# Distance attention: VectorE's clip as a maximum with a bank of PSUM, and GpSimd's second product without its wait for that clip

## What is computed

```python
scores = einsum('bhid,bhjd->bhij', qh, kh) / sqrt(DH)
p = softmax(where(maskb, scores, -1e32)) * maskb
cum, tot = cumsum(p, -1), sum(p, -1, keepdims=True)
pos = abs(idx[None, :] - idx[:, None])
dist_scores = sqrt(clip((tot - cum) * pos, 0.0, None))
gamma, diff = -softplus(gammas), exp(sigmoid(pdiff))
total_effect = clip(exp(dist_scores * gamma * diff), 1e-05, 100000.0)
scores = where(maskb, scores * total_effect, -1e32)
out = einsum('bhij,bhjd->bhid', softmax(scores), vh)
```

## Time and profile before

| what | us |
|---|---|
| median of 3 runs | 3223.43 |
| lowest, highest | 3220.07, 3230.75 |
| the profiled execution | 3222.4 |
| its span in the profile | 3220.3 |

### The profile page before, as it was taken

The page is one execution under the profiler, slowest core; times in us unless marked ns, Lnnn a source line. Parts: engine busy times, 40 slices in busy tenths (PEclk is TensorE's granted clock), DMA queues, the critical chain, the costliest instruction groups (busy, mean ns, idle before and its releaser), DMA issues. The chain is left out here.

```text
span 3220.3 us, 46152 instructions
## 1 busy us (share of the span) xinstructions
PE 2755.0 (86%) x14900; PEld 1548.8 (48%) x14900; DVE 1879.3 (58%) x4757; ACT 1721.1 (53%) x2884; POOL 852.0 (26%) x957
## 2 busy tenths in 40 slices
PE   7899869959999999556699988999867888888887
PEld 4233349824444454322322257999533444444453
DVE  6677551165555655303688640111569999999963
ACT  3565421146555555101277632333159999999963
POOL 4100020020000000001300021000447888888840
PEclk8899989979999999788899999999987999999989
DMA  5111156510000000694312145999250010000011
GB/s 172 47 51 50 48 180 218 195 58 1 1 1 1 1 1 1 264 423 191 96 49 64 45 157 222 341 348 343 86 174 11 21 27 17 22 21 20 18 30 49
DMA packets 161813, 327.00 MB, mean 102 GB/s; under 512 B 29408, under 2 KB 128480, under 8 KB 138208
## 3 DMA queue, kind: packets, MB, share of 16 engines
q1 hardware_dynamic: 152128, 304.78, 27.0%
q0 software_dynamic: 4608, 12.59, 1.2%
q10 hardware_dynamic: 4896, 7.35, 0.7%
HBM read 275.22 MB, written 49.28 MB: 101 GB/s over the span
## 5 line engine op out<-in xcount | busy, mean ns | idle before, releaser
L2987 DVE TENSOR_TENSOR_SCAN L3x_behind<-L3x_first_exp,L3x_beside_scan 128x513 f32<-128x513 f32 x256 | 309.7, 1210 | 0.0
L2867 POOL TENSOR_TENSOR L3x_fade<-L3x_behind,L3x_apart 128x1024 f32<-128x1024 f32 x128 | 280.8, 2194 | 68.6 <-DVE L3x_behind L2987 45.0
L1320 ACT ACTIVATE L1x_probs<-L1x_scores,L1x_neg_max 128x512 f32<-128x512 f32 x256 | 173.5, 683 | 218.7 <-DVE L1x_neg_max L1372 218.7
L1372 DVE TENSOR_REDUCE L1x_neg_max<-L1x_scores 128x2 f32<-128x1024 f32 x128 | 156.6, 1224 | 143.9 <-PE L1x_scores L1220 143.9
L2905 ACT ACTIVATE L3x_first_exp<-L3x_scores,L3x_nm 128x512 f32<-128x512 f32 x256 | 226.9, 886 | 9.9 <-DVE L3x_nm L2979 9.8
L1653 ACT ACTIVATE L2f_hiddenT<-L2f_hidden_ps,L2f_b1s 128x128 f32<-128x128 f32 x320 | 99.9, 363 | 208.1 <-PE L2f_hidden_ps L1588 208.1
L2933 ACT ACTIVATE L3x_probs_T<-L3x_probs_tp 128x512 f32<-128x512 f32 x256 | 203.0, 794 | 12.6 <-PE L3x_probs_tp L2795 12.5
L796 DVE CUSTOM_DVE_ANT_0 L0x_masked_scores<-L0x_s,L0x_mask_q 128x512 f32<-128x512 f32 x256 | 167.1, 685 | 61.5 <-issue 55.6
L2913 ACT ACTIVATE L3x_fade<-L3x_fade,L3x_rl 128x512 f32<-128x512 f32 x256 | 198.2, 938 | 0.0
L791 DVE TENSOR_REDUCE L2x_neg_max<-L2x_s 128x1 f32<-128x512 f32 x256 | 164.7, 686 | 42.4 <-PE L2x_s L687 42.1
L2979 DVE TENSOR_REDUCE L3x_nm<-L3x_scores 128x1 f32<-128x512 f32 x256 | 173.1, 676 | 17.9 <-PE L3x_scores L2772 17.2
(11 more groups left out here) (537 smaller groups left out, 6265.1 us busy)
## 6 DMA issues: line engine op xcount, KB each, us to landing
L2f_w1s<-in_L_w SPq DMA_DIRECT2D x40, 1024.0 KB, 7.6
L2f_w2s<-in_L_w SPq DMA_DIRECT2D x40, 1024.0 KB, 6.3
L1f_w1s<-in_L_w SPq DMA_DIRECT2D x32, 1024.0 KB, 16.0
L1f_w2s<-in_L_w SPq DMA_DIRECT2D x32, 1024.0 KB, 10.5
L0f_w1s<-in_L_w SPq DMA_DIRECT2D x16, 1024.0 KB, 6.0
L0f_w2s<-in_L_w SPq DMA_DIRECT2D x16, 1024.0 KB, 5.1
L0x_q_stack<-L0x_q_parts SPq DMA_DIRECT2D x96, 64.0 KB, 2.6
L0x_k_stack<-L0x_k_parts SPq DMA_DIRECT2D x96, 64.0 KB, 2.7
```

What stands on the lines that cost most here:

```text
L1320: nc.scalar.activation(p[:, n % 3, h, :], s[:, n % 2, h, :], ACT.Exp, bias=nmax[:, n % 4, h:h + 1], accum_out=den[:, n % 4, h:h + 1]).then ...
L2867: nc.gpsimd.tensor_tensor(fz[:, f:f + 2, :], bs[:, fb:fb + 2, 0:S], w, ALU.mult).then_inc(y_done, 1)
L2987: nc.vector.tensor_tensor_scan(bs[:, f, :], ex[:, t, :], beside[:, 0:1].to_broadcast([P, S + 1]), 0.0, ALU.add, ALU.bypass).then_inc(f_don ...
```

## The change

VectorE's clip, a maximum with the number 1e-5, becomes a maximum of two tensors, where the second is the first column of the bank `beside`, repeated over the row. For that the bank is set to 1e-5 instead of 0. GpSimd's `body` loses the wait for `clip_done` ahead of the second product.

```diff
@@ the body of GpSimd
                     for half in range(2):
-                        if half and there(k + (-1)):
-                            pool.wait_ge(clip_done, k)
                         if there(k + 1):
                             distance(k + 1, (i + 1) % 8, half)
@@ VectorE, before the loop
-                nc.vector.memset(beside[:], 0.0)
+                nc.vector.memset(beside[:], 1e-5)
@@ VectorE's clip
                     f = (i % 4) * TB
                     dve.wait_ge(eff_done, u + 1)
-                    nc.vector.tensor_scalar(fz[:, f:f + 2, 0:S], fz[:, f:f + 2, 0:S], 1e-5, None, ALU.max
+                    nc.vector.tensor_tensor(fz[:, f:f + 2, 0:S], fz[:, f:f + 2, 0:S],
+                                            beside[:, 0:1].unsqueeze(2).to_broadcast([P, 2, S]), ALU.max
                                             ).then_inc(clip_done, 1)
```

## The result

The changed kernel takes 3228.99 us in the median of 13 runs, the kernel before 3223.43 us beside it: a ratio of 1.0017 with a 95% interval of [1.0009, 1.0024]. That is 5.6 us more, within 0.3% and yet clear of zero. The forecast was 11 us more; the range of 3227 to 3243 us holds the result, near its lower end. The profiled span is 3226.2 us against 3220.3.

The account below looks back on a forecast made before the run. ScalarE was taken as the bound, at 10.57 us a unit against VectorE's 10.26, with VectorE becoming it after the change. Terms of +6.4, +2.2, -0.5 and +2.9 us made +11.0, for a median of 3234.4 us; range 3227 to 3243.

Parts of the forecast that it names:

- (a): 54 units from the seventh to the 61st clip: VectorE becomes the bound at 10.79 us a unit, +6.4 us.
- (b): Five units before the seventh clip, already on VectorE's floor: 0.44 us more each, +2.2 us.
- (c): Stage ends: first clip no longer loses 1 us to GpSimd, taken as -0.5 us; drain counts 0.
- (d): Seven falls of TensorE's clock to 1.2 GHz in the 54 units: 0 to 0.8 us each, taken as +2.9 us.
- The removed wait is worth nothing: GpSimd's second product: its wait for the scan always contains the wait for the clip, so removal brings 0.
- No blocking of the new clip: VectorE's new clip is not held up by GpSimd: all 64 alike at 1.2 us, none near 2 us.
- ScalarE still shows no idle time: Sign of being wrong in the new profile; expected instead was some 0.2 us of ScalarE idle time a unit.
- the sum's fixed part, +8.1 us: The forecast's terms for the 54 units, five units before and first clip, without the clock falls: +8.1 us.
- the 9.7 us that count as slower: About 0.3% of the whole kernel's time, the least difference a measurement can tell from no change.
- the rival of the hidden cost: Attention stage: VectorE's floor only 10.74 us and clock falls perhaps free, so 3226 to 3229 us; chance 0.27.

Follow-up runs that it names:

- the copy moved: Kernel before with the copy of the turned outputs (once for two units) moved from ScalarE to VectorE: 3214.03 us against 3222.54, ratio 0.9975.
- the quarter on GpSimd: Kernel before with the turned-outputs copy on VectorE and a quarter of VectorE's clip (256 of 1024 elements) on GpSimd: ratio 1.0021.
- the first two experiments: Kernel before without GpSimd's wait for the clip: ratio 0.9997; changed kernel with that wait put back: ratio 1.0016.

## Why the prediction was right, and where it was off

- *VectorE becomes the bound, at 10.79 us a unit* (a): right. 10.787 measured, +6.1 us for +6.4. The clip was taken at 1.22 us with a step of 1.13; it has 1.203 and 1.13. The rate of the reduction and the two-tensor rows was the right upper end. So was the rule of the Trainium skill, "VectorE: DVE Perf Modes", "Why PSUM operands drop a tier": the trace agrees, with 1.203 us for 1024 elements. Whether it is the operand in PSUM or the second tensor as such that costs the rate, no run here separates; the two-tensor row without PSUM in the earlier trace rows has the same rate.
- *The first five units* (b): +2.2 us measured, +2.2 forecast.
- *The first clip* (c): 0.5 us less to the second clip, as forecast; another 0.7 us came from the stretch before the first clip, which I had not counted and cannot assign.
- *Seven dips at 0 to 0.8 us each, taken as +2.9 us* (d): this is the step that failed (and 2.9 is 0.1 above the middle of its own range). It measured 0: there was no dip at all in the 54 units. I had counted the same seven dips into a ring whose waits had moved. As to their price, where VectorE has a unit 0.2 us or more above ScalarE's floor, as here, dips cost 0 to 0.14 us; at 0.07 us above it they cost 0.5. Why they went stays open. The basis I gave, "56.4 us in 48 waits", was misread: the list of waits has 55.0 us in 66, and only the waits of 1.23 to 1.32 us ahead of the seven dips bear it out.
- *The drain, 0* (c): it gave 1.7 us back. Before, a dip lies in it, and in the same place after there is none. The windows of before, then of the changed kernel:

```profile
3086.60:3089.80 3.20, 3.20 (x12) 2.11 (x13) 2.35 (x12) 3.20 (x5) 2.48 (x4) 0.50 0.00 0
```

```profile
3086.60:3089.80 3.20, 2.87 (x20) 2.04 (x21) 3.20 (x9) 3.20 (x7) 2.96 (x4) 1.00 0.01 3
```

  In the run with the wait put back, the same drain takes 26.0 us with a dip in it, against 24.7 here and 25.0 with the copy moved, both without one. But it takes 25.6 us with half of the clip in the new form and 26.3 us with the quarter on GpSimd, and these have no dip in it either. So the dip is a likely cause and not a shown one.
- *The removed wait is worth nothing*: right, shown by the first two experiments.
- *No blocking of the new clip*: right, 1.197 to 1.215 us for all 64.
- *ScalarE's idle time*: a sign that failed. "ScalarE still shows no idle time" stood among the signs of being wrong, and it came: 2.3 us in 54 units, not 0.2 us in each. The bound had moved all the same, as starts show. The sign was a bad one, and so was the first reading of the prediction, that ScalarE is the bound because it is busy all but 2 us: it is so in both kernels. Its floor of 10.57 us, taken from starts, holds. The overlap of 0.09 us is VectorE's; ScalarE's records overlap by more.
- *The chances*: the sum's fixed part, +8.1 us, lay below the 9.7 us that count as slower, and the 2.9 us of the dips alone carried the forecast beyond. With them at zero, 0.3 us less in (a), 1.7 in the drain and 0.7 before the first clip, and 0.4 more at the end, some 5.9 us are left. The time lies at the upper edge of the rival of the hidden cost (3226 to 3229 us). That rival was right that dips may cost nothing and wrong on the floor, for which it had 10.74 us. My range reached down to it, so it held; without the two stretches that I had at nothing the time would be 2.4 us higher and inside too.

## What to carry to other kernels

When two engines share a ring, put a number on each one's floor from the distance between starts where it is packed; the difference is what an edit may cost before it shows, here 0.31 us of 10.6. Take the floors from starts, not from busy time. Moving 0.3 us from one engine to the other won 8.5 us, but most of that by the dips that went with it, which no floor foretells. Do not carry stalls of the old ring over into the new sum unasked: another engine as the bound may hide them, and their number can change either way. A step onto an engine with idle time can still lose, if its instructions block the bound engine's at the wrong moment; look at when it runs, not only at how much room it has.

## What the runs showed that I had not expected

- TensorE's clock does not follow its idle time. It had 576.35 - 509.16 = 67 us of idle time in 54 units before, at seven dips, and 76 us after, at none. The longest single wait, 1.3 against 0.7 us, looked like the reason, but the other runs do not bear it out (idle time by the windows of the 54 units, the longest wait by the lists of waits):

| run | bound | us a unit | TensorE idle, us a unit | its longest wait, us | dips |
|---|---|---|---|---|---|
| before | ScalarE | 10.67 | 1.24 | 1.3 | 7 |
| one idle write | ScalarE | 10.66 | 1.26 | 1.3 | 7 |
| four idle matmuls | ScalarE or TensorE | 10.66 | 0.79 | 0.7 | 2 |
| three at one tile | ScalarE | 10.66 | 0.79 | 0.7 | 4 |
| half of the clip | VectorE, just | 10.66 | 1.16 | 0.6 | 3 |
| changed kernel | VectorE | 10.79 | 1.41 | 0.7 | 0 |
| changed, without the mask | VectorE | 10.79 | 2.11 | 1.2 | 3 |
| two idle writes | VectorE | 10.84 | 1.50 | 1.1 | 0 |
| copy on VectorE | VectorE | 10.56 | 1.13 | 1.0 | 0 |
| copy, and a quarter on GpSimd | VectorE | 10.77 | 1.34 | 1.3 | 8 |

  Neither the bound, nor the idle time, nor the longest wait sorts the runs. What makes the clock fall stays open.
- The blocking between VectorE's number clip and GpSimd's product costs 0.05 us a unit where they barely overlap, nothing with the copy moved (a mean step of 0.600 us), and 0.34 us a unit when GpSimd's clip is then 0.67 us longer. The form with PSUM is free of it, but at 1.13 us a step it pays more than either.
